# Exponents, Relu and masked u changed in place in PSUM, and new instruction orders, in a fused GNN kernel on one core

## The reference

```python
for l in range(2):                                   # block 0, called L0 in the kernel
    u_left, u_right = h @ (h @ W_left[l].T).T / temper, h @ (h @ W_right[l].T).T / temper   # per graph
    u = u_left * triu(adj) + u_right * triu(adj, 1).T
    e = exp(u) * adj
    ctx = (e / (e.sum(2) + 1e-10)) @ (h @ W_lin[l].T + b_lin[l])
    h = relu(layer_norm(ctx, ln_a[l], ln_b[l]))      # std with ddof=1, eps 1e-3 added to it
x = layernorm(x + h)
q, k, v = x @ Wq.T, x @ Wk.T, x @ Wv.T + bv          # block 1, called L1: 12 heads of 32
s = q @ k.T * 384 ** -0.5 + 2 * adj                  # a row that is all zero gives p = 0
p = softmax(s)
x = layernorm(x + (p @ v) @ Wo.T + bo)
```

## Time and profile before

| | |
|---|---|
| median of 3 runs (lowest, highest) | 2750.87 us (2749.57, 2752.33) |
| the profiled execution: its time, its span | 2750.55 us, 2748.8 us |
| busy share: PE, DVE, ACT, POOL | 94%, 86%, 68%, 60% |
| PE's weight loads | 56% |
| mean granted clock of PE | 0.986 of full |
| chain that ended last, by engine | DVE 41%, PE 38%, issue 10%, ACT 5%, POOL 3%, DMA 2% |
| DMA engines, mean | 38.7%, 88 GB/s |

### The profile page before, as it was taken

The page is one execution under the profiler, slowest core; times in us unless marked ns, Lnnn a source line. Parts: engine busy times, 40 slices in busy tenths (PEclk is TensorE's granted clock), DMA queues, the critical chain, the costliest instruction groups (busy, mean ns, idle before and its releaser), DMA issues.

```text
span 2748.8 us, 70524 instructions
## 1 busy us (share of the span) xinstructions
PE 2581.7 (94%) x25152; PEld 1527.9 (56%) x25152; DVE 2356.8 (86%) x8074; ACT 1863.5 (68%) x4395; POOL 1655.0 (60%) x1686
## 2 busy tenths in 40 slices
PE   6999999999999999999999999999999999999976
PEld 3555555555555555555555555555555555555543
DVE  4788988889888889888889888889888898888885
ACT  4666776667776667776667776667766677766664
POOL 3556665565666565766565755566655656665644
PEclk9999999999999999999999999999999999999986
DMA  4235343344443343443343443343433433433333
GB/s 157 53 88 104 71 101 86 76 96 82 93 92 92 69 106 73 101 90 85 79 104 70 105 92 74 90 101 73 98 90 77 96 83 92 93 92 71 84 79 67
DMA packets 557742, 242.33 MB, mean 88 GB/s; under 512 B 506704, under 2 KB 539472, under 8 KB 557392
## 3 DMA queue, kind: packets, MB, share of 16 engines
q1 hardware_dynamic: 557392, 237.83, 38.7%
HBM read 86.77 MB, written 25.17 MB: 41 GB/s over the span
## 4 chain that ended last, share of the span: by engine, by line
DVE 41%; PE 38%; issue 10%; ACT 5%; POOL 3%; DMA 2%; SPq 1%; DVEq 0%; ACTq 0%; POOLq 0%
PE psum L1322 36%; DVE nT_lo L883 4%; DVE rs L948 3%; DVE s L912 3%; DVE z L1093 2%; DVE x L1121 2%; DVE y L979 2%; DVE s L923 2%; DVE z L1102 2%; DVE xTin L1157 2%; PE psum L1446 2%; DVE st L987 2%; DVE hl_raw L896 1%; DMA pT_lo<-s 1%; DVE yst L1048 1%
## 5 line engine op out<-in xcount | busy, mean ns | idle before, releaser
L657 ACT ACTIVATE w<-s,nmax 128x128 f32<-128x128 f32 x1536 | 477.6, 391 | 29.6 <-DVE nmax L912 29.4
L1322 PE MATMUL psum<-hT_hi,w_hi 128*128 128x512 f16 x1152 | 439.9, 382 | 34.2 <-DVE nT_lo L883 20.8
L1322 PE MATMUL psum<-hT_lo,w_hi 128*128 128x512 f16 x1152 | 438.3, 380 | 0.0
L1322 PE MATMUL psum<-hT_hi,w_lo 128*128 128x512 f16 x1152 | 437.8, 380 | 0.0
L596 ACT ACTIVATE nT_hi<-psum 128x512 f16<-128x512 f32 x384 | 220.7, 590 | 303.8 <-PE psum L1322 303.8
L912 DVE CUSTOM_DVE_ANT_0 s<-psum,adj 128x128 f32<-128x128 f32 x1536 | 345.6, 284 | 23.0 <-PE psum L1446 19.3
L446 POOL TENSOR_TENSOR hl_lo<-hl_raw,hl_hi 128x384 fp32r<-128x384 f32 x256 | 238.7, 938 | 192.5 <-ACT hl_hi L596 192.5
L518 POOL TENSOR_TENSOR fold<-s 128x768 f32<-128x768 f32 x128 | 243.2, 1900 | 152.6 <-DVE nmax L912 137.2
L883 DVE SCALAR_TENSOR_TENSOR nT_lo<-psum,nT_hi 128x512 f16<-128x512 f32 x384 | 251.8, 683 | 29.5 <-ACT nT_hi L596 29.1
L596 ACT ACTIVATE z<-psum,rden 128x384 f32<-128x384 f32 x256 | 134.2, 575 | 184.5 <-DVE rden L1034 184.5
L529 POOL TENSOR_TENSOR s<-w,s 128x512 f16<-128x512 f32 x128 | 164.1, 1282 | 145.3 <-ACT s L596 145.3
(11 more groups left out here) (132 smaller groups left out, 7792.3 us busy)
## 6 DMA issues: line engine op xcount, KB each, us to landing
xTin<-xT SPq DMA_DIRECT2D x32, 768.0 KB, 4.4
xres<-x SPq DMA_DIRECT2D x32, 768.0 KB, 5.5
out<-y SPq DMA_DIRECT2D x128, 192.0 KB, 2.0
adjm<-adjM SPq DMA_DIRECT2D x32, 384.0 KB, 5.2
adjT_sb<-adjT SPq DMA_DIRECT2D x32, 256.0 KB, 4.7
adj<-adj SPq DMA_DIRECT2D x32, 256.0 KB, 3.3
x<-weights SPq DMA_DIRECT2D x4, 576.0 KB, 4.6
pT_hi<-s SPq DMA_TRANSPOSE x128, 3.8
```

The costliest lines, as they stand in the source:

```text
L657: last = nc.scalar.activation(w[:, m], s[b % 2][:, m], ACT.Exp, bias=nmax[b % 2][:, m:m + 1], scale=-1.0)
L1322: last = mm(dst, a, b, start=(i == 0), stop=(i == total - 1))
```

## The change

1. **Exponents stay in PSUM.** `exps` writes its result over the scores in banks 4 to 7 and not to `w`. `pt` is four instructions of 384 (one a bank) on ACT and four on DVE for each graph, all reading PSUM; POOL has none. The halves go to two new buffers `p16`, and `READ["s"]` becomes `pt_lo`: a scores bank is free only after the exponents' low half is taken. `scores` of graph b+1 on PE waits for that.
2. **th and u in place.** The Relu in float32 is written over its PSUM bank, u is masked in its bank (the right third goes to a small SBUF tile, so two instructions for one), and `exp_u` reads PSUM. Those banks are held till `th_lo` and `e_raw`.
3. **The test for a dead row** moves from `live_of` to `rs_of`: reciprocal to PSUM, two small products, a maximum (four instructions for two); `live_of` keeps the sum alone.
4. **The last norm on POOL.** `fin` is one POOL instruction with pointer scalars, (y-mean)·rstd; ACT's and DVE's part go. The `x1_norm` of graphs 2 and 3 moves from ACT to POOL. `+eps` for these norms moves from DVE to POOL, and the variance factor of z is folded into `inv_std`. DVE's small -mean·rstd products go everywhere.
5. **New orders** for all five engines' lists and a new bank rotation. On PE `pv(3)` is now first in the pass, ahead of `nl(0,0)`. SP's list is reordered too.

Of the diff, the core (the last function stands in POOL's part):

```diff
-                    last = nc.scalar.activation(w[:, m], s[b % 2][:, m], ACT.Exp, bias=nmax[b % 2][:, m:m + 1],
+                    last = nc.scalar.activation(psum[:, SC[j], c * TOK:(c + 1) * TOK], s[b % 2][:, m], ACT.Exp, bias=nmax[b][:, m:m + 1],
                                                 scale=-1.0)
...
-                act.wait_ge(fold1.sem, p.upto(fold1, b + 1))
-                act.wait_ge(p_ok.sem, p.upto(p_ok, TILES * b + r + 2))
-                copy(p_hi[b % 2][:, part], w[:].rearrange("p h t -> p (h t)")[:, part]).then_inc(pt_hi.sem, 1)
+                act.wait_ge(p_ok.sem, p.upto(p_ok, TILES * b + j + 1))
+                copy(p16[b % 2][:, 0, KB * TOK * j:KB * TOK * (j + 1)], psum[:, SC[j], 0:KB * TOK]).then_inc(pt_hi.sem, 1)
...
+                nc.vector.tensor_tensor(p16[b % 2][:, 1, part], psum[:, SC[j], 0:KB * TOK], p16[b % 2][:, 0, part],
+                                        ALU.subtract).then_inc(pt_lo.sem, 1)
...
-        READ = {"nl0": nl_lo[0], "nl1": nl_lo[1], "hl0": hl_sum[0], "hl1": hl_sum[1], "u0": u_read[0], "u1": u_read[1],
-                "c0": z_ok[0], "c1": z_ok[1], "th": th_hi, "qk": qkr_lo, "v": v_sum, "s": s_ok,
+        READ = {"nl0": nl_lo[0], "nl1": nl_lo[1], "hl0": hl_sum[0], "hl1": hl_sum[1], "u0": e_raw[0], "u1": e_raw[1],
+                "c0": z_ok[0], "c1": z_ok[1], "th": th_lo, "qk": qkr_lo, "v": v_sum, "s": pt_lo,
                 "pv": o_ok, "to": to_lo, "po": y2_ok}
...
+                nc.vector.reciprocal(rcp, src[:, :, HEAD]).then_inc(rcp_ok.sem, 1)
+                nc.vector.scalar_tensor_tensor(rs[b % 2][:], total[b][:], 0.0, rcp, ALU.is_gt, ALU.mult)
+                nc.vector.scalar_tensor_tensor(peak, nmax[b][:], 0.0, rcp, ALU.is_lt, ALU.mult)
+                nc.vector.tensor_tensor(rs[b % 2][:], peak, rs[b % 2][:], ALU.max).then_inc(rs_ok.sem, 1)
...
+            def fin(run, b):
+                pool.wait_ge(y2pow_ok.sem, p.upto(y2pow_ok, b + 1))
+                nc.gpsimd.tensor_scalar(y2[:, b % 2], y2[:, b % 2], mv2[:, b % 2, 0:1], rstd2[:, b % 2:b % 2 + 1],
+                                        ALU.subtract, ALU.mult).then_inc(fin_ok.sem, 1)
```

More of the change, by code:

```diff
@@ L19 @@
 BIG = 3.0e38
+UNBIAS = (FEAT / (FEAT - 1.0)) ** 0.5
 class Signal:
@@ L535, in y2_power, with x1_norm @@
                     return
+                pool.wait_ge(y2mv_ok.sem, p.upto(y2mv_ok, b + 1))
+                var = var2[:, b % 2:b % 2 + 1]
+                nc.gpsimd.tensor_scalar(var, mv2[:, b % 2, 1:2], 1e-5, None, ALU.add).then_inc(y2var_ok.sem, 1)
                 pool.wait_ge(y2var_ok.sem, p.upto(y2var_ok, b + 1))
-                power(rstd2[:, b % 2:b % 2 + 1], var2[:, b % 2:b % 2 + 1], 1, y2pow_ok)
+                power(rstd2[:, b % 2:b % 2 + 1], var, 1, y2pow_ok)
+            def fin(run, b):
+                p = run.of("fin", b)
+                if p is None:
+                    return
+                pool.wait_ge(y2pow_ok.sem, p.upto(y2pow_ok, b + 1))
+                nc.gpsimd.tensor_scalar(y2[:, b % 2], y2[:, b % 2], mv2[:, b % 2, 0:1], rstd2[:, b % 2:b % 2 + 1],
+                                        ALU.subtract, ALU.mult).then_inc(fin_ok.sem, 1)
+            def x1_norm(p, b):
+                if not p.l1:
+                    return
+                if b == 2:
+                    pool.wait_ge(ypow_ok.sem, p.upto(ypow_ok, 1))
+                nc.gpsimd.tensor_scalar(x1[:, b], x1[:, b], ymv[:, b, 0:1], yrstd[:, b:b + 1],
+                                        ALU.subtract, ALU.mult).then_inc(x1_half.sem, 1)
             def body(p):
@@ L667, in exp_u @@
                                       (second, second, first), (second, first, second)):
-                        nc.scalar.activation(e[j, two, i], uLR[h][j, :, src], ACT.Exp).then_inc(e_raw[l].sem, 1)
+                        last = nc.scalar.activation(e[j, two, i], tri(l, h)[j, :, src], ACT.Exp)
+                    last.then_inc(e_raw[l].sem, 1)
             def round_e(p, l, h):
@@ L765, in body @@
                 hl(p, 0, 0)
-                exp_u(p, 0, 0)
+                setup(p, 5)
+                setup(p, 6)
                 hl(p, 0, 1)
-                round_e(p, 0, 0)
-                exp_u(p, 0, 1)
                 hl(p, 0, 2)
                 hl(p, 0, 3)
+                exp_u(p, 0, 0)
+                exp_u(p, 0, 1)
+                round_e(p, 0, 0)
+                qk(p, 0)
                 round_e(p, 0, 1)
+                qk(p, 1)
+                setup(p, 7)
+                xt(p, 0)
                 ctx(p, 0, 0)
@@ L829, in body @@
                 exps(p, 3, 2)
+                to(p, 0)
+                pt(p, 3, 0)
+                pt(p, 3, 1)
+                exps(p, 3, 3)
+                exp_u(p, 1, 0)
+                exp_u(p, 1, 1)
+                pt(p, 3, 2)
+                pt(p, 3, 3)
+                round_e(p, 1, 0)
+                round_e(p, 1, 1)
+                hl(p, 1, 3)
                 v(p, 3)
-                exps(p, 3, 3)
-                pt(p, 3, 0)
-                exp_u(p, 1, 0)
                 to(p, 1)
-                pt(p, 3, 1)
-                hl(p, 1, 2)
-                pt(p, 3, 2)
-                round_e(p, 1, 0)
-                exp_u(p, 1, 1)
-                fin(p, 0)
-                hl(p, 1, 3)
                 to(p, 2)
-                round_e(p, 1, 1)
                 ctx(p, 1, 0)
@@ L847, in body @@
                 ctx(p, 1, 3)
-                fin(p, 1)
             def head():
```

523 lines of the change are left out of this document (236 added, 287 removed).

## The result

The changed kernel takes **2855.52 us** (median of 3 runs, 2852.57 to 2856.3). Its ratio to the kernel before is 1.0378, with a 95% interval of 1.0354 to 1.0401. That is 3.8% slower, 105 us, where 1.7% faster was forecast. Its profiled execution spans 2854.6 us.

What follows compares the result with a forecast made beforehand. PE was taken to set the pace, DVE close behind: 78.0 us of matmuls plus 2.8 of listed and 1.0 of other waits made 81.8 a pass, 1.4 gained over 31 passes, so 2705 us, range 2670 to 2735.

Steps and rivals of the forecast that it cites:

- the engines' loads: Per-pass work on DVE, ACT and POOL after the change; DVE -0.7 us of work and -3.3 of waiting, POOL even.
- Even: POOL's load per pass: 4 x 1.28 us go; six affines (3.7 at most) and five adds (about 1.5) come.
- The loads therefore do not decide: Conclusion from DVE, ACT and POOL loads per pass: the dependences decide the time instead.
- The walk of the start of the pass: From pv(3): no wait there, by 1.0 us; po(3)'s to_lo behind seven DVE instructions, about 0.3; ctx(0,0) waits some 0.3.
- 2.8 at listed places: PE's waits per pass: 1.0 from graph 0 to 1, 1.2 at ctx(1,0) and ctx(1,2), 0.3 at po(3), 0.3 at ctx(0,0).
- 1.0 for all others: Allowance per pass for PE waits that the walk misses, those not above 0.3 us; bounds 0 and 2.3.
- graph 0 to 1: Between their scores, ACT and DVE's chain takes 9.8 us, PE's work 8.8; PE waits 1.0, mostly at hl(1,0).
- just in time: At the start of the pass, the transpose of x1 arrives for qk(0) with no wait counted.
- the refill behind waits: Of PE's 5.2 us over the matmuls per pass before, 3.1 is idle time seen; the rest is the pipe's refill.
- the 78.0 us of matmuls as floor: PE's unchanged matmuls per pass sum to 78.0 us, so only 5.2 us a pass can be won.
- rival 3: Scores bank cycle: PE waits at scores(1), (2), (3) for the lo part; at 1 us a round 2800; chance 0.26.
- Rival 4: Gain given back: late DVE list uncovers pv(3), or fin and x1_norm on POOL hold up DVE; 2740 to 2760; chance 0.14.

Runs made afterwards that it cites:

- one_ptr: Changed kernel with the mean's pointer replaced by constant 1.0 in all six POOL affines, the inverse deviation's pointer kept; 2852.23 us, ratio 1.0367.
- imm: Changed kernel with all six POOL affines multiplying twice by constants 1.0, so those norms are left out; 2751.69 us, ratio 1.0004.
- dve_th0: dve_early_pv with fin(0) on DVE two steps earlier, behind den(1,1), and th(0) one step earlier, ahead of scores(0,2); 2764.99 us, ratio 1.0056.
- both2_w: both2 with exponents written over the scores' copy in SBUF, scores banks free once DVE has read them, dead-row test left out; 2898.93 us, ratio 1.0536.
- dve_early_pv: Changed kernel with all six affines on DVE, y2_power(3) and fin(3) early, pv(1) behind nl(1,5), rs_of(1) behind pt(2,3); 2807.8 us, ratio 1.0206.
- both2_swap: both2 with store(3) moved behind turn_p(2) on SP's queue; 2808.24 us, ratio 1.0206.
- both2: Changed kernel with all six affines on ACT, fin(0) placed behind ctx(1,3); 2810.12 us, ratio 1.0214.
- before_poolfin: Kernel before with only the last norm of four graphs as one POOL affine each, ACT's and DVE's parts removed, old orders; 3007.57 us, ratio 1.0928.

## Why the prediction was wrong, point by point

- **The step that failed** is in the engines' loads: "six affines come, priced by the 512-wide tensor_scalar of 0.62, 3.7 at most". They take 1.66 and 1.76 us, 10.1 a pass. That row multiplies twice by constants; these subtract and multiply, with pointers. one_ptr shows that one pointer fewer changes little, and the subtraction was not tried apart. "At most" was no bound: no row of POOL had a pointer scalar, so the far end should have come from its dearer rows: six at the 1.28 us of its 512-wide tensor_tensor are 7.7 us. imm puts the whole 104 us on this term, which reaches the time through `po(3)`'s wait and, by the estimate above, for some 16 of it through the clock that falls behind such waits; the forecast put the clock at nothing.
- **The second step that failed** is its consequence, "Even", and "The loads therefore do not decide". With 10.1 us of affines POOL is still only 63% busy. What decides is where they stand: fin(0) and fin(1) directly ahead of z_power(1), whose result DVE needs before `to(3)`. The walk of the start of the pass had DVE's seven instructions ahead of to(3)'s low half, but not the POOL chain ahead of those, 1543.38 to 1552.25.
- **The gain itself** was also missing. With the price taken away (imm) the pass is 83.28 us, against the 81.8 forecast and 83.22 before. The forecast's 3.8 us over the matmuls were 2.8 at listed places and 1.0 for all others. imm has 5.3. Of the listed, 1.5 came: ctx(1,0) waited 0.6 for 1.0, scores(2) and (3) nothing; for graph 0 to 1 it had 1.0 at hl(1,0), and 0.8 came, but at v(1), for the bank of th(0), where dve_th0 shows that the wait could be cut without the time following. So the term that was too small is the 1.0: pv(1), which the walk doesn't list, and qk(0), "just in time", cost 0.8 and 0.7 a pass, both for a transpose's DMA, and another 2.2 stand in no record of a wait. The forecast knew that remainder as the refill behind waits; why it is this large was not tried.
- **Right:** the 78.0 us of matmuls as floor; `pt` on DVE at 0.55 and ACT's copies at 0.48; the exponents within 40 ns (363 for 391, on the cheap side); rs_of's products at 0.17 without stalls; pv(3) without a DMA wait in fourteen of sixteen passes; u's two parts (422 and 282 ns); DVE's load, which went down: 1090.16 us of 1331.50 in the window above, 70.8 a pass, for the 72.4 that the sum gives (73.1 - 0.7).
- **The rivals.** The outcome is on the other side, but not by rival 3: PE does not wait for the exponents' low half at any `scores` of the sixteen passes (only in the last passes, which lack block 0, does it wait for it, twice, 9.0 us in all), and undoing the in-place exponents in both2_w makes it worse. Rival 4 named the right instructions (`fin` and x1_norm on POOL) with the wrong mechanism and price (six of at most 0.6). Its mechanism exists in another form: DVE's fin(0) held for POOL's mask in dve_early_pv, and `p`'s low half at 829 ns in both2_w.
- **The two rules cited.** The Trainium skill ("VectorE: DVE Perf Modes", section on the TRN2 errata) would make the PSUM reads dearer, since it gives VectorE a higher fixed cost with a PSUM source. The low half reads PSUM at 384 columns in 548 ns, and out of SBUF with no POOL instruction beside it in 546 (both2_w), so no such cost is seen here. What the Trainium skill ("SBUF — State Buffer", section Who interferes with whom) says of two SBUF inputs beside GpSimd is borne out: that low half takes 932 ns on the mean when a POOL instruction is already running, and 550 when it begins first. The same section of the Trainium skill says that a tensor_scalar can contend with GpSimd too, where its operands meet the conditions that it names; fin(0), a tensor_scalar out of and into SBUF, took 1.51 us when `mask` was already running.
- **Still open:** why the versions with both affines on ACT stay 51 to 58 us above imm. There ACT waits for POOL's `nmr`, and DVE's `po` waits 42.6 us in the span for a store in both2_swap (3.9 in imm), the shape that cost dve_early_pv 41 us. That it is the same chain is argued, not tried.

## What to carry to other kernels

A price comes from a row with the same operation and operands, not only the same kind and width: a scalar by pointer and a constant, a subtraction and a product, are two instructions as long as no row says otherwise, and where no row has the form, both ends of the range stay wide. When a step moves to another engine, follow what it now stands in front of, on that engine and on the DMA queue that waits for it: one store or one norm in the wrong place cost 41 to 107 us here, while the work itself was 0.5 us. When a loss has one cause, take its cost away first (constants in place of pointers), since that also shows what the rest of the change is worth; and keep the operation the same while doing it, or the cause of the price stays open. Where TensorE's waits reach some 2 us, read the granted clock behind them too.

## What the hardware showed that was not expected

- On GpSimd a tensor_scalar of 128x384 takes 513 ns with two constants (two products), 1583 with one pointer and 1656 with two (a subtraction and a product); 561, 1680 and 1762 in x1_norm. On VectorE the last takes 472 (median).
- A VectorE tensor_tensor with both inputs in SBUF takes 546 to 550 ns at 384 columns if it is alone or begins first, and 932 on the mean if a GpSimd instruction is already running (both2_w); with one input in PSUM it takes 549, beside GpSimd or not (both2).
- ScalarE's exponent of 128 columns takes 363 ns into PSUM and 391 to 394 into SBUF.
- In before_poolfin the granted clock of TensorE fell to half after it had stood idle for 2.23 us; the first matmul behind the wait, in the timeline of PE:

```profile
1123.12 1.11 PE L1318 MATMUL psum<-ident,z 128*128 128x128 f32 x4 [2.23 <-DVE z L1078]
```

Windows of 1 us (same columns as above; the clock is third from the end):

```profile
1122.00:1123.00 1.00, 0.00 (x0) 0.00 (x0) 1.00 (x4) 0.00 (x0) 0.00 (x0) 0.99 0.00 0
1123.00:1124.00 1.00, 0.88 (x4) 0.71 (x4) 1.00 (x3) 0.00 (x0) 0.00 (x0) 0.50 0.00 0
...
1129.00:1130.00 1.00, 1.00 (x5) 0.49 (x4) 1.00 (x8) 1.00 (x3) 0.00 (x0) 0.59 0.00 0
1130.00:1131.00 1.00, 1.00 (x8) 0.59 (x6) 1.00 (x7) 0.41 (x1) 0.35 (x1) 1.00 0.00 0
```

It ran at the lower level (1.2 GHz) from 1123 for some 6.8 us (six windows at 0.50, and 0.82 of the seventh, (1 - 0.59) / 0.5) and then came back to 2.4 GHz. In the kernel before no such fall is seen: the granted clock of the window of the earlier trace rows is 1.00. Waits as long as this one are so paid for twice in that kernel, and, less often, in the changed one.
